# Reordering the elementwise work of the first thirteen slots on VectorE, ScalarE and GpSimd in a fused attention and feed-forward block

## The reference, cut to what matters

```
x = layernorm(x) * w + b + tanh(cond @ lin_w.T + lin_b);  x = x * w + b
n = gamma_a * rmsnorm(x) + beta_a
x = x + alpha_a * (softmax(0.25 * q @ k.T) @ v) @ W_o.T          # q, k, v = n @ W.T
n = gamma_f * rmsnorm(x) + beta_f
x = x + alpha_f * ((silu(n @ gate.T) * (n @ hidden.T)) @ out_w.T + out_b)
```

## Time and profile before

| | |
|---|---|
| median of 3 runs | 977.93 us |
| the profiled execution: time / span | 978.47 us / 976.6 us |
| TensorE matmul busy | 930.5 us (95%) |
| VectorE busy | 718.6 us (74%) |
| ScalarE busy | 615.2 us (63%) |
| GpSimd busy | 584.3 us (60%) |
| TensorE's mean granted clock | 0.989 |

### The profile page before, as it was taken

How to read it: one execution, slowest core, us unless ns; L and a number is a source line. 1 busy time by engine, 2 the same in 40 slices (tenths; PEclk the granted TensorE clock), 3 DMA queues, 4 the chain that set the end, 5 groups by cost and what they waited for, 6 DMA issues and landing times.

```text
span 976.6 us, 28344 instructions
## 1 busy us (share of the span) xinstructions
PE 930.5 (95%) x11164; PEld 895.2 (92%) x11164; DVE 718.6 (74%) x1355; ACT 615.2 (63%) x1732; POOL 584.3 (60%) x531
## 2 busy tenths in 40 slices
PE   5567999999999999999999999999999999999997
PEld 4456999999999999999999999999999999998997
DVE  6677777787777778777777777777777776777654
ACT  4455776677667667766766776676677667666432
POOL 4467757666575766657576665757666575544320
PEclk9789999999999999999999999999999999999999
DMA  6000001000000100010000001001000000000000
GB/s 231 30 24 23 2 12 34 13 23 13 29 18 13 34 13 23 12 33 14 13 34 13 23 13 34 13 12 35 12 23 13 13 13 12 13 12 12 13 11 22
DMA packets 20930, 23.33 MB, mean 24 GB/s; under 512 B 1216, under 2 KB 20288, under 8 KB 20800
## 3 DMA queue, kind: packets, MB, share of 16 engines
q1 hardware_dynamic: 20800, 21.54, 6.8%
HBM read 13.15 MB, written 8.39 MB: 22 GB/s over the span
## 4 chain that ended last, share of the span: by engine, by line
PE 90%; DVE 3%; POOL 2%; issue 2%; ACT 1%; DMA 0%; SPq 0%; ACTq 0%; DVEq 0%; POOLq 0%
PE psum L301 18%; PE psum L303 18%; PE psum L302 18%; PE psum L513 6%; PE psum L515 6%; PE psum L514 6%; PE psum L447 5%; PE psum L423 4%; PE psum L463 3%; PE psum L352 2%; PE psum L333 2%; PE psum L341 1%; POOL probs L1117 1%; PE psum L345 1%; PE psum L308 0%
## 5 line engine op out<-in xcount | busy, mean ns | idle before, releaser
L301 PE MATMUL psum<-xf_hi,ffn_hi 128*128 128x256 f32 x1024 | 289.7, 283 | 3.4 <-ACT probsT L922 1.6
L303 PE MATMUL psum<-xf_hi,ffn_lo 128*128 128x256 f32 x1024 | 285.9, 279 | 0.0
L302 PE MATMUL psum<-xf_lo,ffn_hi 128*128 128x256 f32 x1024 | 285.9, 279 | 0.0
L914 ACT ACTIVATE probs<-psum,least 128x64 f32<-128x64 f32 x928 | 205.2, 354 | 56.1 <-DVE least L643 55.5
L301 PEld LDWEIGHTS psum<-xf_hi,ffn_hi 128*128 128x128 f32 x1024 | 192.2, 188 | 4.7 <-issue 2.8
L1117 POOL TENSOR_TENSOR probs<-probs,inv_sum 128x512 f32<-128x512 f32 x128 | 134.2, 1050 | 101.3 <-DVE inv_sum L664 100.6
L303 PEld LDWEIGHTS psum<-xf_hi,ffn_lo 128*128 128x128 f32 x1024 | 192.3, 188 | 0.0
L302 PEld LDWEIGHTS psum<-xf_lo,ffn_hi 128*128 128x128 f32 x1024 | 192.1, 188 | 0.0
L943 ACT ACTIVATE prod_hi<-late 128x512 fp32r<-128x512 f32 x128 | 83.8, 655 | 114.8 <-DVE late L722 112.6
L714 DVE SCALAR_TENSOR_TENSOR late<-tanh,psum 128x512 f32<-128x512 f32 x128 | 86.7, 678 | 77.9 <-ACT tanh L937 77.9
L513 PE MATMUL psum<-prod_hi,ffn_hi 128*128 128x256 f32 x512 | 143.2, 280 | 0.9 <-DVE prod_lo L728 0.9
(11 more groups left out here) (103 smaller groups left out, 2204.3 us busy)
## 6 DMA issues: line engine op xcount, KB each, us to landing
out_t_dram<-x_res SPq DMA_DIRECT2D x31, 256.0 KB, 2.2
xin<-x_dram SPq DMA_DIRECT2D x15, 512.0 KB, 4.0
w_raw<-attn_w_dram SPq DMA_DIRECT2D x1, 1024.0 KB, 6.8
x_res<-gate_w_dram SPq DMA_DIRECT2D x1, 1024.0 KB, 9.5
late<-hidden_w_dram SPq DMA_DIRECT2D x1, 1024.0 KB, 11.5
w_raw<-out_w_dram SPq DMA_DIRECT2D x1, 1024.0 KB, 6.4
xin<-x_dram SPq DMA_DIRECT2D x2, 256.0 KB, 2.9
k_heads<-mod_w_dram SPq DMA_DIRECT2D x1, 320.0 KB, 4.7
```

The lines of the kernel that those rows point to most:

```text
L301: pe.matmul(out, stat_hi, mov_hi, start=first, stop=False)
L302: pe.matmul(out, stat_hi, mov_lo, start=False, stop=False)
L303: return pe.matmul(out, stat_lo, mov_hi, start=False, stop=last)
L914: op = act.activation(probs[g % 4][:, h * SEQ:(h + 1) * SEQ], scores[g % 2][:, h // 2, h % 2], ACT.Exp, bias=least[g % 2][:, h:h + 1], sca ...
```

## The change

No instruction of TensorE or of the DMA queue is moved. On the other three engines the same work is put in another order in slots 0 to 12; no instruction is added or dropped.

- VectorE, slot 0: `scale_a(1)` goes ahead of the two `find_least` and `centre`. Slot 12: `merge_stats` of block 3, before at the end of slot 11, comes after `make_residual`.
- ScalarE: in slot 0 `split_hi_a(1)` goes ahead of the exponentials. In slots 4, 8 and 12 `keys_out` goes ahead of the exponentials. In slots 6 and 10 `split_hi_a` (before in slots 7 and 11) comes ahead of `probs_out` and `values_out`. In slot 12 `square_f(1)` comes after `keys_out` and not first.
- GpSimd: the powers of `inverse_rms` in slots 1, 5 and 9 go ahead of `apply_gamma_a` and `apply_gamma_f`; `split_lo_a` in slots 0, 2, 6 and 10 comes ahead of a `normalise_probs`; `token_rstd` and the first `normalise_tokens` of block 2 go from slot 4 to slot 5, behind the power and the gamma.

The diff, cut to these:

```
 VectorE
+                if s == 0:
+                    scale_a(1)
                 if s % 2 == 0:
                     for g in (s, s + 1):
                         if is_seq(g):
                             find_least(g)
                             if wide(g):
                                 centre(g)
-                    if s == 0:
-                        scale_a(1)
...
                     make_residual(grp + 2)
+                if s == FFN_AT:
+                    merge_stats((grp + 3) // 2, (grp + 3) // 2 + 2)
...
-                    if j == 3:
+                    if j == 3 and grp != 2:
                         merge_stats((grp + 4) // 2, (grp + 4) // 2 + 2)
 ScalarE
-                if j == 0 and is_part(grp - 2) and not wide(s):
+                if j == 0 and is_part(grp - 2) and s > FFN_AT:
                     square_f(grp - 2)
...
+                if s == 0:
+                    split_hi_a(1)
+                if wide(s) and j == 0 and s > 0:
+                    keys_out(grp + 1)
+                if s == FFN_AT:
+                    keys_out(grp + 1)
+                    square_f(grp - 2)
                 if s % 2 == 0 and is_seq(s):
                     exponentials(s)
-                    if wide(s) and j == 0 and s > 0:
-                        keys_out(grp + 1)
...
+                if j == 2 and PSEQ <= s < FFN_AT:
+                    split_hi_a(grp + 2)
                 if s % 2 == 0 and 0 < s < FFN_AT:
                     probs_out(s - 2)
                     probs_out(s - 1)
...
-                if j == 3 and s >= 0 and is_part(grp + 2):
+                if j == 3 and (s == 3 or s >= FFN_AT) and is_part(grp + 2):
                     split_hi_a(grp + 2)
 GpSimd
                 if s == 0:
                     apply_beta_a(1)
+                    split_lo_a(1)
...
                         normalise_probs(g)
-                if s == 0:
-                    split_lo_a(1)
+                        if g == s and j == 2:
+                            split_lo_a(grp + 2)
...
-                if j == 0 and s >= 0 and is_part(grp + 2):
+                if j == 0 and s >= FFN_AT and is_part(grp + 2):
                     apply_gamma_a(grp + 2)
...
                 if j == 1 and is_group(grp):
                     inverse_rms(grp)
+                if j == 1 and 0 <= s < FFN_AT:
+                    apply_gamma_a(grp + 2)
+                    if is_part(grp - 2):
+                        apply_gamma_f(grp - 2)
...
-                if j == 0 and grp % 2 == 1 and 1 <= (grp + 3) // 2 < NBLK:
+                if j == (grp == 1) and grp % 2 == 1 and 1 <= (grp + 3) // 2 < NBLK:
                     token_rstd((grp + 3) // 2)
-                if grp % 2 == 1 and 2 <= (grp + 3) // 2 < NBLK:
+                if grp == 1 and j == 1:
+                    normalise_tokens((grp + 3) // 2, 0)
+                if grp % 2 == 1 and 2 <= (grp + 3) // 2 < NBLK and not (grp == 1 and j == 0):
                     normalise_tokens((grp + 3) // 2, j)
```

More of the change, by code:

```diff
@@ L1003, in _ @@
                 if s == 0:
-                    split_hi_a(1)
                     values_out(0)
@@ L1017, in _ @@
                         split_ffn_weights(c)
-                if j == 0 and is_part(grp + 1) and not 0 <= s < FFN_AT:
+                if j == 0 and is_part(grp + 1) and not 0 <= s <= FFN_AT:
                     keys_out(grp + 1)
@@ L1152, in _ @@
                     apply_gamma_a(grp + 2)
-                if j == 0 and is_part(grp - 2):
-                    if not wide(s):
-                        sum_squares_f(grp - 2)
+                if j == 0 and is_part(grp - 2) and not wide(s):
+                    sum_squares_f(grp - 2)
                     apply_gamma_f(grp - 2)
-                if j == 0 and s >= 0 and is_part(grp + 2):
+                if j == 0 and s >= FFN_AT and is_part(grp + 2):
                     apply_gamma_a(grp + 2)
-                    if not wide(s):
-                        sum_squares_a(grp + 2)
+                    sum_squares_a(grp + 2)
                 if j == 1 and is_group(grp):
                     inverse_rms(grp)
+                if j == 1 and 0 <= s < FFN_AT:
+                    apply_gamma_a(grp + 2)
+                    if is_part(grp - 2):
+                        apply_gamma_f(grp - 2)
                 if j == 2 and is_part(grp - 2):
@@ L1168, in _ @@
                     normalise_probs(s)
-                if j == 3 and is_part(grp + 2) and s != -1:
+                if j == 3 and is_part(grp + 2) and s != -1 and not 0 <= s < FFN_AT:
                     split_lo_a(grp + 2)
```

## The result

The changed kernel takes 970.57 us (median of 4 runs, 969.66 to 970.98) against 978.12 (4 runs, 977.55 to 980.22): ratio 0.9917, 95% interval 0.9902 to 0.9932, so it is faster: the medians are 7.6 us apart, and the interval is 6.6 to 9.6 us. (The ratios here are of the means of the executions, the times are medians.) The profiled execution took 969.66 us with a span of 967.8, which is 8.8 us less than before's. The forecast was 967.6, in a range of 964.6 to 971.8.

The account below looks back on a forecast made before the run. Matmuls bind the kernel after about 100 us; before that a serial chain round all engines. Tanh 10.85 us earlier less 0.5 for the clock is 10.35: 978.47 to 968.1 profiled, median forecast 967.6, range 964.6 to 971.8.

Parts of the forecast that it names:

- Slot 0 and 1: Front end's start: keys 7.5 us earlier, but products only 1.05; power of slot 1 at 37.3 us, 6.35 earlier.
- Slots 2 to 4: Engines go round as before, so the first minimum of slot 4 comes at 46.4 us, 6.35 earlier.
- The term for the merge: Statistics merge ahead of slot 4's minimum: -7.45 if free of GpSimd, -5.3 if two operations collide, -6.35 taken.
- The 0.5 charged: Low clock on queries and first turned products of slot 2: up to 2 us on TensorE, 0.5 charged.
- Slots 4 to 6: Products 6.6 us earlier, beta of slot 6 at 59.0, 7.0 earlier; under 1 of 8.8 us of waits gained.
- Slots 6 to 8: `probsT` 7.75 us earlier, minima of slot 8 7.35, squares 8.7 with the keys' copy ahead of the exponentials.
- The 0.4 charged for `ffn_lo`: Slots 6 to 8: `ffn_lo` beside a busy GpSimd could lose 0 to 1.2 us; 0.4 taken.
- Slots 9 to 11: Transposes 10.8 us earlier, `scale_a(4)` at 75.2, 9.6 earlier; 0.2 lost, keys at 83.4, 9.4 earlier.
- Slot 12: Tanh 3.8 us after the keys' end, before 5.35: at 88.8 us, 10.85 earlier.
- only the early steps: Rival: waits and collisions eat what slots 4 to 12 add; slot 1's 6.35 us stays, 971.6 us; chance 0.15.
- The low clock: Rival: low clock at three places, slot 2 in full and slot 12's keys, 970.3 us; chance 0.12.
- The others: Rivals: nothing left, 977.9 us, 0.03; slower, 1.2 GHz through slots 1 to 12, 982, 0.03; better, 964.6, 0.06.

Follow-up runs that it names:

- The filler: Changed kernel plus extra identity transposes on TensorE in slots 1, 2, 5, 6, 9 and 10, output unchanged: 969.69 us, ratio 0.9903.
- the kernel with beta first: Changed kernel with beta of slot 6 ahead of the layer norm's second tile on GpSimd: 969.04 us, ratio 0.9900.

## Why the prediction was right, and where its terms were off

The mechanism was right: the dense stretch passes on what the front end gains, and the chain is the one followed. Measured from the common start, so without the 0.26 us by which this profile starts later:

- **The ground.** The prediction reads nine tenths from the sixth slice on; its row has them from the fifth, which begins at 97.7 us. The forecast does not hang on it.
- **Slot 0 and 1.** -6.35 forecast, -6.38 measured at the power. The 7.2 us of the low part did not pass on, as said.
- **Slots 2 to 4.** -6.35 forecast, -5.57 measured. The term for the merge was "-7.45 to -5.3, I take -6.35". The merge started at -5.88, so 0.5 was gone before it, and it lost 0.31 itself: the two long operations took 2.11 us and before 1.78. The 0.5 is the low clock: it made the queries 1.1 us longer and the copy and the exponential behind them late. The filler gives 0.54 back here. The 0.5 charged was for that, and it was charged once for the whole front end.
- **Slots 4 to 6.** Beta -7.0 forecast, -6.12 measured: the step itself was right (-0.65 against -0.55), the debt is slot 4's. Of the 8.8 us of waits for the power little is gained up to beta, as said. But the moves of the powers in slots 1, 5 and 9 together are not small: undone, they cost 3.5 us.
- **Slots 6 to 8.** Minima -7.35, measured -6.90; squares -8.7, measured -8.05. The reason given for the last 1.35 us was wrong. It is not the keys' copy's place in front of the exponentials (undone, nothing changes) but the earlier low part, which lets the keys end before ScalarE needs them (undone, the squares are 2.6 us later, up to 1.2 of it by the clock). `probsT` moved by 6.88 us, which is beta's 6.12 and 0.76 as forecast (0.75). The 0.4 charged for `ffn_lo` did not come: it ran in 0.69 again.
- **Slots 9 to 11.** Beta of slot 10 -8.72 against -9.6 for the scaling; the step is right within 0.3.
- **Slot 12.** Tanh -9.59 against -10.85. The keys started at 84.86, which is -8.21 against -9.4: slots 10 and 11 gave back 0.5 us and not 0.2, with GpSimd's last product at 1.49 us beside a split of weights on VectorE. From there to the tanh it takes 5.5 us, as forecast (1.52 and 3.8), against 6.86 before. Of slot 12's edits only the square's was undone by a run; which of the others makes the 1.4 us is argued in the prediction and not shown.
- **Behind it.** This step failed: "everything behind it in before's rhythm". 0.86 us is given back by slot 14, by the square moved behind the keys' copy: with the square ahead again, the tanh gains 0.42 and slot 14 gains 1.28, and the difference is these 0.86.
- **Total.** The profiled execution took 969.66 us against 968.1 forecast. The median lies 0.9 above that execution and before's 0.35 below its own; this 1.3 us is spread between executions. Part of it is the start. In slot -3 the projection starts its matmuls 0.21 us apart, as in the stretches with a granted clock of 0.50, and then 0.12 apart. In the profile of before:

```profile
23.06 0.41 PE L303 MATMUL psum<-xn_hi,w_lo 128*128 128x256 f32 x1
23.27 0.41 PE L301 MATMUL psum<-xn_hi,w_hi 128*128 128x256 f32 x1
...
23.66 0.28 PE L303 MATMUL psum<-xn_hi,w_lo 128*128 128x256 f32 x1
23.78 0.28 PE L301 MATMUL psum<-xn_hi,w_hi 128*128 128x256 f32 x1
```

In that of the kernel with beta first the change comes at about 25.6 us. (The rows of stretches write a granted clock of 1.00 for both, so the level is read from the spacing.) The power of slot -1 is at 25.97 in the one and at 26.91 in the other, though nothing in front of it was changed. How often each occurs was not measured.

The measured 970.57 lies in the stated range, but outside the forecast's own 965.8 to 969.8, and nearer to two rivals (971.6 and 970.3) than to the forecast. By the total alone the forecast could not be told from them. The milestones do it: "only the early steps" would have kept 6.35 us at the tanh, and it is 9.59. The low clock came true in part and in other places than named (slots 2, 5 to 6 and 9 to 10, not the keys of slot 12); the filler gets 0.74 us back at the tanh, and the rival charged 2.7, so that its total comes so near is chance. The others are refuted by the result. (The forecast's own range does not quite follow from its terms: 1.5 us for merge and `ffn_lo` free and 1.85 for both blocked give 966.1 to 969.5.)

## What to carry to other kernels

In a front end where in-order engines pass one part round, follow the milestone that carries the chain on, and not the longest wait: 7 us less wait of the projections was 1 us at the next link. Judge a move by which engine's queue stands behind the instruction that it releases, too: the power of slot 5 freed no time on its own engine, but TensorE's queue stood behind it, and up to 1.4 us of the gain by slot 8 went with it. Before a difference between two orders is put down to the order, compare the granted clock of the same projections in both. Tiny operations of VectorE are best placed where GpSimd idles, and a filler of useless matmuls can pay in a stretch of short bursts (0.74 us at the tanh in one kernel, 1.46 at slot 14 in another).

## What was not expected of the hardware

- Merge operations of 128x4 took 0.15 to 0.17 us beside an idle GpSimd and up to 1.27 beside a busy one. The rule of the Trainium skill that the prediction cites ("SBUF — State Buffer", section "Who interferes with whom") speaks of two SBUF inputs, and the long operations of before and of the changed kernel have two. But in other kernels operations with one were as long: 1.27 us (`mean`, in the kernel with the high and low parts behind the turned products) and 1.24 us (in the one with the powers behind the gammas).
- In the changed kernel TensorE was busy 1.79 of the 4 us from 52 to 56, and the granted clock was 0.86 there and 0.50 from 56 to 60. A change that leaves the bursts as short shifts the low stretches to other slots, and they decide 0.5 to 1.2 us of a step's worth.
